# Row sums of a two-path 3x3 convolution: one vector instruction replaced by two transfers

## What is computed

```
mask = repeat(mean_8x8(x) >= 0.05)
x_high = where(mask, x, EPS);  x_low = where(mask, EPS, x)
y = conv3x3(quant(x_high, s_high, 8 bits), quant_w(w_high, 8 bits))
  + conv3x3(quant(x_low,  s_low,  4 bits), quant_w(w_low,  4 bits))
```

## Time and profile before

| What | Value |
|---|---|
| median of three runs | 652.44 us (650.45 to 653.19) |
| the profiled execution's own time | 653.09 us |
| its span, first to last instruction | 651.3 us |
| TensorE (PE) busy | 626.5 us, 96% |
| VectorE (DVE) busy | 593.7 us, 91% |
| ScalarE (ACT) busy | 483.9 us, 74% |
| GpSimd (POOL) busy | 9.7 us, 1% |
| mean granted TensorE clock | 0.994 |
| transfers | 104.07 MB, mean 160 GB/s; packets took 41.9% of 16 engines' span |
| chain that ended last | PE 95%, ACT 2%, DVE 1%, DMA 1% |

### The profile page before, as it was taken

How to read it: one execution, slowest core, us unless ns; L and a number is a source line. 1 busy time by engine, 2 the same in 40 slices (tenths; PEclk the granted TensorE clock), 3 DMA queues, 4 the chain that set the end, 5 groups by cost and what they waited for, 6 DMA issues and landing times.

```text
span 651.3 us, 10766 instructions
## 1 busy us (share of the span) xinstructions
PE 626.5 (96%) x3714; PEld 360.8 (55%) x3714; DVE 593.7 (91%) x805; ACT 483.9 (74%) x491; POOL 9.7 (1%) x30
## 2 busy tenths in 40 slices
PE   3779999999999999999999999999999999999996
PEld 1345555555555555555555555555555555555554
DVE  7889999999999999999999999999999999999933
ACT  6669877787787787787778778777778877877542
POOL 3200000000000000000000000000000000000000
PEclk9889999999999999999999999999999999999999
DMA  6244555334355433445543434553343554331122
GB/s 270 99 156 142 199 199 197 150 123 177 141 197 197 184 126 142 182 155 197 197 154 125 172 148 190 197 194 129 139 179 148 197 197 160 129 162 63 78 99 100
DMA packets 14409, 104.07 MB, mean 160 GB/s; under 512 B 1728, under 2 KB 1728, under 8 KB 10432
## 3 DMA queue, kind: packets, MB, share of 16 engines
q1 hardware_dynamic: 14400, 103.95, 41.9%
HBM read 52.56 MB, written 51.38 MB: 160 GB/s over the span
## 4 chain that ended last, share of the span: by engine, by line
PE 95%; ACT 2%; DVE 1%; DMA 1%; issue 0%; DVEq 0%; SPq 0%
PE psum L335 95%; DMA wraw_l<-w_low 1%; ACT rounded_h L449 0%; ACT psum L484 0%; ACT wT_l L466 0%; DVE pooled L618 0%; PE psum L321 0%; DVE w_max_l L577 0%; ACT wT_h L466 0%; DVE ybuf L712 0%; DVEq L63 0%; DVE wq_l L600 0%; DVE wint_l L584 0%; DVE upper L696 0%; DVE wq_l L589 0%
## 5 line engine op out<-in xcount | busy, mean ns | idle before, releaser
L484 ACT ACTIVATE psum<-psum,ratio 128x1344 f32<-128x1344 f32 (+2 forms) x159 | 174.4, 1097 | 123.7 <-PE psum L335 122.7
L335 PE MATMUL psum<-plane_l,wT_l 128*128 128x448 f16 (+1 forms) x1164 | 207.8, 328 | 0.0
L335 PE MATMUL psum<-plane_h,wT_h 128*128 128x448 f16 (+1 forms) x1164 | 205.5, 326 | 0.0
L335 PEld LDWEIGHTS psum<-plane_l,wT_l 128*128 128x128 f16 x1164 | 114.3, 98 | 77.8 <-issue 3.0
L335 PEld LDWEIGHTS psum<-plane_h,wT_h 128*128 128x128 f16 x1164 | 113.4, 98 | 76.6 <-issue 1.7
L712 DVE SCALAR_TENSOR_TENSOR ybuf<-psum,out_scale_h,shared 128x448 f32<-128x448 f32 (+1 forms) x194 | 111.2, 601 | 20.0 <-PE psum L335 9.7
L618 DVE TENSOR_REDUCE pooled<-xbuf 128x49 f32<-128x3136 f32 (+2 forms) x33 | 109.3, 3313 | 0.0
L449 ACT ACTIVATE rounded_l<-xbuf,inv_act_l 128x1568 int16<-128x1568 f32 (+1 forms) x64 | 101.7, 1592 | 4.5 <-DMA xbuf<-x 4.5
L505 ACT ACTIVATE shared<-psum,bias,out_scale_h 128x448 f32<-128x448 f32 (+1 forms) x128 | 86.3, 674 | 23.2 <-PE psum L335 22.6
L449 ACT ACTIVATE rounded_h<-xbuf,inv_act_h 128x1568 int16<-128x1568 f32 (+1 forms) x64 | 101.9, 1594 | 0.0
L335 PE MATMUL psum<-rowsum_l,wT_l 128*128 128x448 f16 (+1 forms) x384 | 87.2, 336 | 2.3 <-ACT wT_l L466 2.3
(11 more groups left out here) (76 smaller groups left out, 340.6 us busy)
## 6 DMA issues: line engine op xcount, KB each, us to landing
xbuf<-x SPq DMA_DIRECT2D x31, 1568.0 KB, 6.6
y<-ybuf SPq DMA_DIRECT2D x32, 896.0 KB, 3.6
y<-ybuf SPq DMA_DIRECT2D x32, 672.0 KB, 4.0
xbuf<-x SPq DMA_DIRECT2D x1, 896.0 KB, 7.6
xbuf<-x SPq DMA_DIRECT2D x1, 672.0 KB, 5.0
wraw_l<-w_low SPq DMA_DIRECT2D x1, 576.0 KB, 3.8
wraw_h<-w_high SPq DMA_DIRECT2D x1, 576.0 KB, 5.9
act_scales<-scales SPq DMA_DIRECT2D x1, 1.0 KB, 1.8
```

Of the source, the lines that this page charges most:

```text
L335: last = nc.tensor.matmul(out, wT[k][:, mat, :], moving(k, p, band, row, dx), start=(k == "l" and j == 0), stop=(j == len(parts) - 1), ski ...
L484: return nc.scalar.activation(banks, banks, ACT.Identity, scale=ratio[:, 0:1])
```

## The change

The row sums of image 0 stay as they are, in two parts on VectorE. For all other images VectorE makes none. Instead GpSimd runs a loop over images 1 to 31, with four transfers in each, from SBUF to SBUF: for each kind one that copies the odd rows of the plane into `rowsum`, and one that adds the even rows to what is there (`accum_op=ALU.add`). The copy of a kind waits until both of its plane's instructions are done; the adding transfer waits until the copy of its kind has landed. TensorE waits for the adding transfer's landing. The two buffers of `plane` and of `rowsum` become halves of one tensor, so that a loop's variable can choose between them. A transfer moves 128 partitions of 1626 elements of 2 bytes: 416,256 bytes, or 406.5 KB.

```diff
-        plane = {k: [sb(f"plane_{k}{p}", [P, PLANE], F16) for p in range(2)] for k in "hl"}
-        rowsum = {k: [sb(f"rowsum_{k}{p}", [P, SUMS], F16) for p in range(2)] for k in "hl"}
+        planes = {k: sb(f"plane_{k}", [P, 2, PLANE], F16) for k in "hl"}
+        plane = {k: [planes[k][:, p, :] for p in range(2)] for k in "hl"}
+        rowsums = {k: sb(f"rowsum_{k}", [P, 2, SUMS], F16) for k in "hl"}
+        rowsum = {k: [rowsums[k][:, p, :] for p in range(2)] for k in "hl"}
...
+        s_rows_copied = {k: sem(f"row_sums_begun_{k}") for k in "hl"}
+        s_rows_summed = {k: sem(f"row_sums_landed_{k}") for k in "hl"}
@@ GpSimd, behind the bias @@
+            def begin_row_sums(k, m, p):
+                pool.wait_ge(s_plane[k], 2 * prepared(m))
+                nc.gpsimd.dma_start(rowsums[k][:, bass.ds(p, 1), :], planes[k][:, bass.ds(p, 1), ODD:ODD + SUMS]
+                                    ).then_inc(s_rows_copied[k], 16)
+
+            def add_row_sums(k, m, p):
+                pool.wait_ge(s_rows_copied[k], 16 * m)
+                nc.gpsimd.dma_start(rowsums[k][:, bass.ds(p, 1), :], planes[k][:, bass.ds(p, 1), PITCH:PITCH + SUMS],
+                                    accum_op=ALU.add).then_inc(s_rows_summed[k], 16)
+
+            pool.wait_ge(s_border[0], BORDERS)
+            pool.wait_ge(s_border[1], BORDERS)
+            with pool.Fori(1, B) as m:
+                p = m % 2
+                begin_row_sums("l", m, p)
+                begin_row_sums("h", m, p)
+                add_row_sums("l", m, p)
+                add_row_sums("h", m, p)
@@ TensorE @@
-            def wait_prepared(signal, n, band):
+            def wait_prepared(k, n, band):
                 if first_image(n):
-                    pe.wait_ge(signal, 1 if band == 0 else 2)
+                    pe.wait_ge(s_rowsum[k], 1 if band == 0 else 2)
                 elif band == 0:
-                    pe.wait_ge(signal, prepared(n))
+                    pe.wait_ge(s_rows_summed[k], 16 * n)
@@ VectorE, body of the first image @@
                     apply_mask("l", m, mp)
-                    row_sums("l", m, mp)
                     out_rows(n, p, 2)
                     apply_mask("h", m, mp)
-                    row_sums("h", m, mp)
                     out_rows(n, p, 3)
@@ VectorE, body of the other images @@
                     apply_mask("l", m, mp)
                     apply_mask("h", m, mp)
-                    row_sums("l", m, mp)
...
                 out_rows(n, p, 0)
-                if ahead > 0:
-                    row_sums("h", m, mp)
                 out_row(n, p, 1, 0)
```

More of the change, by code:

```diff
@@ L348, in low @@
                 new = not (first_image(n) and band < 2)
-                wait_prepared(s_rowsum["l"], n, band)
+                wait_prepared("l", n, band)
                 if new:
@@ L373, in high @@
                 g = BANDS * n + band
-                wait_prepared(s_rowsum["h"], n, band)
+                wait_prepared("h", n, band)
                 if fast(n, band):
@@ L653, in apply_mask, with row_sums @@
                         ALU.mult).then_inc(s_plane[k], 1)
-            def row_sums(k, n, p, q=None):
-                a0, a1 = (0, BY) if q is None else PART[q]
+            def row_sums(k, q):
+                p = 0
+                a0, a1 = PART[q]
                 at, size = a0 * POOL // 2 * PITCH, (a1 - a0) * POOL // 2 * PITCH + 2
-                if early(n):
-                    dve.wait_ge(s_border[p], BORDERS)
-                dve.wait_ge(s_plane[k], 2 * prepared(n, 1 if q is None else q))
+                dve.wait_ge(s_border[p], BORDERS)
+                dve.wait_ge(s_plane[k], 2 * prepared(0, q))
                 flat = plane[k][p][:, :]
@@ L728, in _ @@
             apply_mask("l", 0, 0, 0)
-            row_sums("l", 0, 0, 0)
+            row_sums("l", 0)
             weights("h")
@@ L732, in _ @@
             apply_mask("h", 0, 0, 0)
-            row_sums("h", 0, 0, 0)
+            row_sums("h", 0)
             low_ratio()
@@ L740, in _ @@
                 apply_mask(k, 0, 0, 1)
-                row_sums(k, 0, 0, 1)
+                row_sums(k, 1)
             def body(i, p, ahead):
```

## The result

The changed kernel took 664.63, 664.76, 665.02 and 665.19 us, median 664.89 us. The kernel before had a median of 652.66 us over four runs. The ratio is 1.019, 95% interval 1.0175 to 1.021: slower by 1.9%. The profiled execution took 664.63 us, with a span of 662.8 us.

A forecast was written before the change was run, and what follows sets the result against it. TensorE's unbroken row of matmuls from image 1 was taken as the bound; a 7.2 us stall there plus 1.7 us of clock loss gave 661.3 us, 1.4% slower. Likeliest case 654.6 to 664.2 us; 8-in-10 range 655 to 700.

The forecast's parts named there:

- The bound: From image 1 on TensorE runs one unbroken row of matmuls, 595.7 us; any delay or gap is paid in full.
- What it removes is worth 0: VectorE loses 62 row-sum instructions, 62 us, all beside TensorE's unbroken row: gain 0.
- One stall, at image 1: TensorE waits for image 1's low sum, queued behind the wait for the high plane: 7.2 us, bounds 2.2 to 10.1.
- g: Time GpSimd takes to issue one transfer: taken as 0.8 us, bounds 0.33 to 0.82; counted twice in image 1's stall.
- a: The adding transfer's time from issue to landing at image 1: taken as 5.9 us, bounds 1.8 to 8.8.
- The clock: After the stall at image 1 TensorE runs 4 us at a granted clock of 0.57: 1.7 us lost.
- Sum: Stall 7.2 plus clock 1.7 is 8.9 us: forecast 661.3 us, own range 654.6 to 664.2, stated range 655 to 700.
- Middle images cost 0: In each later image the low sum's route takes 9.3 us of 11.7 us of slack, 2.4 us to spare.
- Image 2, no stall: Image 2's high plane is ready at 59.3, ten us before TensorE comes to it at 69.3: no stall.
- Rival 1: Transfers become the bound: once the route exceeds 11.7 us, gaps stand before later images, 681 or 747 us; chance 0.29.
- Rival 2: Not measurably slower: image 1's gap stays under 3.3 us, perhaps without clock loss, 654.6 to 655.7 us; chance 0.07.
- Rival 3: Faster: VectorE's relief of 2.0 us reaches TensorE's idle time before image 1, 650.4 us; chance 0.03.

The follow-up runs named there:

- e2: The changed kernel, but image 1's row sums stay on VectorE and the transfers begin with image 2: 651.60 us, ratio 1.0003 to the kernel before.
- e3: Row sums of images 0 and 1 on VectorE, those of images 2 to 31 left out, without GpSimd's loop: 651.39 us, ratio 1.0002 to the kernel before.
- e4: The changed kernel with GpSimd's order low copy, low addition, high copy, high addition: median 663.56 us, ratio 1.021 to the kernel before.
- e1: The changed kernel, but SyncE issues the load of image 4 only after both sums of image 1 have landed: 658.48 us, ratio 1.010 to the kernel before.
- e5: The changed kernel with both adding transfers made plain copies of the same bytes: 660.95 us, ratio 1.015 to the kernel before.
- e6: Image 1's sums on VectorE, and from image 2 three small serial copies ahead of each low addition: 799.79 us, ratio 1.227 to the kernel before.
- e7: Image 1's sums on VectorE, transfers from image 2, and band 2 put on band 3's scheme: 641.31 us, ratio 0.985 to the kernel before.
- e8: The kernel before, all row sums on VectorE, with band 2 put on band 3's scheme: 669.00 us, ratio 1.027 to the kernel before.

## Why the prediction was right, and where its sizes were off

- **The bound.** One unbroken row of matmuls from image 1 on: shown by the window after and by e2. All that delays its start is paid in full, and was.
- **What it removes is worth 0.** Shown by e3, 1.0002, for images 2 to 31. The amount was mis-sized, without effect: VectorE lost 51.1 us and not 62, 0.82 for each of the 62 instructions, whose 0.97 to 1.01 us overlap with their neighbours'.
- **One stall, at image 1, behind the wait for the high plane.** Shown: one gap, gone in e2, when image 1's sums stay on VectorE, and 8 us shorter in e4, where the low addition no longer stands behind the high copy.
- **g, the issue.** Taken at 0.8; the copies were issued in 0.57 us and the additions in 0.90. The addition was issued 1.31 us behind the plane, and its 11.0 us to landing count from there, so 1.31 stands where 2g put 1.6. That is near, but for another reason: 0.65 us pass between the plane and the first issue (46.93 to 47.58), which the prediction did not have, and 0.66 to the next issue.
- **a, the addition's landing at image 1.** This is the term that was mis-sized: 5.9 taken, 11.0 measured, beyond even the upper bound of 8.8. I took it from a 576 KB load that had others beside it. Here the load, a store, both additions and the copies of image 2 stood together for 10 us at a share of 1.01 (e1: 6.8 us of it), and an addition asks more of the engines than its bytes (e5: 4.9 us of it; the two overlap). The windows of before showed that the engines were 0.90 busy for six microseconds from 53 on the earlier trace rows; I should have summed the queue's work there and not read a single transfer's time. I also named the load wrongly: it is that of image 4, not 3; nothing hangs on it.
- **The clock.** 1.7 taken, 2.1 measured. Over the five kernels with such gaps the loss was 1.3 to 2.7 us (e5, e4), for gaps of 3.9 to 11.9 us, and it does not follow the length. Behind e4's gap of 1.5 us nothing was lost (62.30 to 65.22 is 2.92 us).
- **Sum.** 8.9 forecast, 14.0 measured (11.9 and 2.1). The median, 664.9, lies 0.7 us above the likeliest case's own range and within the stated one.
- **Middle images cost 0.** Shown by e2. The margin was 5.4 us and not 2.4, since on engines that are free a copy landed in 2.7 us and a low addition in 4.0.
- **Image 2, no stall.** It came out, but not for the reason given. The prediction saw ten microseconds between plane and demand and did not follow the route. The route took 12.3 us here and was covered by image 1's own delay; in e2, without that delay, it took 10.0 us and was in time by under 0.2 us. That was luck.
- **Rival 1** did not occur. Its mechanism is real once the route is longer than the slack (e6): each gap shortens the next, as stated. The equal gaps did not come; they alternate.
- **Rivals 2 and 3.** Rival 2 falls with the gap of 11.9 us. Rival 3 falls in the changed kernel's own rows: without the low row sum VectorE idled 1.63 us for the shared tile instead of 0.51, and it began the high plane 1.84 us ahead of TensorE's last transposes (45.08 to 46.92), as before (47.97 to 49.80 is 1.83).
- **The Trainium skill's fit** ("DMA: Bandwidth & Descriptors", the gpsimd path's anatomy), 2.95 us for a copy of this size, agrees with the 2.7 us measured on free engines. For the low addition it gave 3.9 with a second read, against 4.0 measured. By it the forecast would have been too small a gap, 4.3 to 5.2 us: right for e1's 5.1, where the engines are free, and wrong for 11.9.
- **The Trainium skill's lock** ("SBUF — State Buffer", who interferes with whom): in the changed kernel the high addition of image 1 was issued at 51.02, within the clip from 50.71 to 51.74, and its issue took 0.88 us as everywhere. That does not speak against a hold, since it ended at 51.90, behind the clip anyway. In e5 and e1 the same issue was the longest of its line: 1.00 us instead of 0.54 (from 52.47, clip to 53.34) and 1.00 instead of 0.87 (from 53.08, clip to 53.95), and both ended 0.13 us behind the clip. So the traces fit the rule, with a hold of 0.1 to 0.5 us; no run tried it by itself. It held back a high addition, and TensorE waited for the low one, so it cost nothing at that gap.

## What to carry to other kernels

Before moving work off an engine, find the one row of work that has no gap, and ask what of the move can start it later or open it; the relief of another engine is worth nothing until it is spent on something that shortens that row, as in e7 against e8. The place to check is the first iteration, where slack that all others have does not yet exist: keeping that one on the old path made a loss of 1.9% into none, though the next image was then in time by under 0.2 us. For a transfer that someone waits for, add up what else is queued on the transfer engines at that moment, and count an accumulating one for more than its bytes.

## What was not expected

A low addition of 406.5 KB from SBUF to SBUF took 4.0 us to land on free engines and 11.0 us beside a 1568 KB load that alone takes 6.6. A copy of 116 bytes per partition took 1.6 us at the least and 5.4 us at the most in e6. The kernel before has two groups of times, some 2.2 us apart, and TensorE's clock in image 0 was at either of its levels at the same place (1.00 and 0.50 in 22.5 to 24), which by itself moves image 1's start by 2.9 us.
